# A transformer layer on 8 cores: the weight statistics move into the attention of the first sequence

## The chip, the cores and the metric

The kernel runs on the 8 NeuronCores of one Trainium2 chip. Every core runs the same program on its own 2 of 16 sequences of 2048 tokens (width 1024); the weights are given whole to each core, and the cores never wait for each other. The metric is the device time of the slowest core, in microseconds (us). Each core has TensorE (PE, matmuls), VectorE (DVE), ScalarE (ACT), GpSimd (POOL, here only a queue for DMA writes) and SyncE (SP, here only a queue for DMA loads), which run side by side and meet by semaphores.

## The reference

One pre-norm layer: attention with 16 heads of 64, then a feed-forward part whose two linear maps work on quantized activations and on weights that are quantized to -1, 0 and 1 with one scale for the whole matrix.

```python
x = x + attention(layernorm(x))            # causal, 16 heads
x = x + ffn(layernorm(x))

def weight_quant(w):                       # w1: 4096x1024, w2: 1024x4096, f32
    scale = 1.0 / clip(mean(abs(w)), 1e-05)
    return clip(round(w * scale), -1, 1) / scale
# ffn: h = bit_linear(x, w1); h = silu(conv1d(h, 3 taps)); bit_linear(h, w2)
```

So the scale of a weight needs the mean of |w| over all of its 4 million elements (16 MB) before a single element can be quantized, and the quantized w1 and w2 are needed only in the feed-forward part.

## The kernel before, in words

The program is written out by hand, once for all engines. A recorder (`Rec`) gathers the instructions of each engine, `emit()` plays them into a block, and `barrier()` makes all five engines meet. Within an engine the order in the text is the order of execution. Semaphores count up (`ve` for DVE, `sc` for ACT, `tn` for PE, `dlx`, `dlb` and others for loads), and `wait` names the count that must be reached. All instructions are played by the recorder's one line, L80, so groups of the profile are told apart by the names of tiles.

The stages, each ended by a barrier:

1. Constants; casting the attention weights to bf16 (`p_wst`, `p_wbf`) and writing them to memory.
2. Weight preparation, for w1 and then for w2, in `wprep`. First the statistics: the matrix is loaded in four pieces of 4 MB into one buffer (`wp_st`), ACT takes the absolute value and sums it up (`wp_j`, `wp_as`), and a short chain over DVE, PE and DVE turns it into the mean and its inverse on all partitions (`c_m`, `c_s`). Then the quantization in 8 blocks of 2 MB: load (`wq_st`), scale on ACT (`wq_f`), clip and round on DVE (`wq_b`), 32 transposes on PE (`wq_tp`), copies on DVE (`wq_sp`), and a write by POOL.
3. For each of the two sequences: A, layer norm and the projections Q, K, V (tiles `a_...`). Then B, attention (`b_...`): a bound for the exponentials, then a loop over 4 blocks p of 512 queries and, within it, over 8 head pairs hp. Such a unit of (p, hp) runs over 4(p+1) key blocks kc: PE makes the logits (`b_lp`), ACT the exponential (`b_pt`), on the last four key blocks (the diagonal ones) DVE zeroes a part and multiplies by a triangle (`c_tri`), and PE multiplies by V (`b_av`). At the end of a unit DVE takes a reciprocal (`b_zr`) and makes eight products (`b_at`). After the 8 units of a p come the output projection of its four row tiles v: PE transposes, DVE casts (`b_tt`), PE multiplies, and DVE adds the residual (`b_xr`) into `x2`. Then C, layer norm, activation quantization and the feed-forward part (`c_...`), whose weights are streamed from what stage 2 wrote.

In a unit the order on DVE is: mask of the first diagonal block, then for each further one memset and mask, then reciprocal and products. PE issues the logits of a key block ahead of the value matmuls of the one before. ACT's exponential of a diagonal block past the first waits for the memset. On SP's queue stage B has 16 loads of `b_xr`, of which each past the second waits for the residual sum of two row tiles before.

Of the kernel before, what the change touches and what calls it, by code (L numbers as in the profile page):

```python
# [7 lines left out]
F32 = mybir.dt.float32  # L8
BF16 = mybir.dt.bfloat16
# [5 lines left out]
D = 1024  # L15
NH = 16
DH = 64
HID = 4096
# [73 lines left out]
def build_program(nseq, S):  # L92
# [66 lines left out]
    def barrier():  # L159
        base = bar.v  # L160
        for e in ENGS:
            er = getattr(r, e)
            bar.inc(er.nop() if e in ("sync", "gpsimd") else er.drain())
        for e in ENGS:
            getattr(r, e).wait_ge(bar.sem, base + 5)
# [76 lines left out]
        barrier()  # L242
        r.emit()

    def wprep(t_w, sw_bc, mw_bc, which):
        wn = which
        nel = HID * D
        with nc.sbuf_tensor(f"wp_st{wn}", [128, 8192], F32) as stg, \
             nc.sbuf_tensor(f"wp_j{wn}", [128, 8192], BF16) as junk, \
             nc.sbuf_tensor(f"wp_as{wn}", [128, 4], F32) as asum, \  # L250
             nc.sbuf_tensor(f"wp_s1{wn}", [1, 4], F32) as s1s, \
             nc.psum_tensor(f"wp_ps{wn}", [128, 512], F32) as ups:
            flat = t_w.rearrange("a b -> (a b)").rearrange(
                "(ci p a) -> ci p a", ci=4, p=128)
            for i in range(4):
                b0 = dl.v
                if i > 0:
                    r.wait(r.sync, sc, sc.v)
                dl.inc(r.sync.dma_start(out=stg[:, :], in_=flat[i]), 16)
                r.wait(r.scalar, dl, b0 + 16)  # L260
                sc.inc(r.scalar.activation(junk[:, :], stg[:, :], AF.Abs,
                                           accum_out=asum[:, i:i + 1]))
            r.wait(r.vector, sc)
            ve.inc(r.vector.reduce_sum(asum[:, 0:1], asum[:, 0:4], axis=AX.X))
            r.wait(r.tensor, ve)
            tn.inc(r.tensor.matmul(ups[0:1, 0:1], asum[:, 0:1], onescol[:, :],
                                   start=True, stop=True))
            r.wait(r.vector, tn)
            ve.inc(r.vector.tensor_scalar(s1s[:, 0:1], ups[0:1, 0:1],
                                          1.0 / nel, 1e-5, ALU.mult, ALU.max))  # L270
            ve.inc(r.vector.drain())
            ve.inc(r.vector.reciprocal(s1s[:, 1:2], s1s[:, 0:1]))
            ve.inc(r.vector.drain())
            r.wait(r.tensor, ve)
            tn.inc(r.tensor.matmul(ups[:, 0:1], ones1f[0:1, :], s1s[0:1, 0:1],
                                   start=True, stop=True))
            tn.inc(r.tensor.matmul(ups[:, 1:2], ones1f[0:1, :], s1s[0:1, 1:2],
                                   start=True, stop=True))
            r.wait(r.vector, tn)
            ve.inc(r.vector.tensor_copy(mw_bc[:, :], ups[:, 0:1]))  # L280
            ve.inc(r.vector.tensor_copy(sw_bc[:, :], ups[:, 1:2]))
            r.emit()
            barrier()

        with nc.sbuf_tensor(f"wq_st{wn}", [128, 2 * 4096], F32) as stg2, \
             nc.sbuf_tensor(f"wq_f{wn}", [128, 4096], F32) as qf, \
             nc.sbuf_tensor(f"wq_b{wn}", [128, 4096], BF16) as qb8, \
             nc.sbuf_tensor(f"wq_sp{wn}", [128, 4096], BF16) as strip, \
             nc.psum_tensor(f"wq_tp{wn}", [128, 1024], BF16) as tpp:
            ve_q = 0  # L290
            dw_s = 0
            ve_g = 0
            sc_q = [0, 0]
            for blk in range(8):
                par = blk % 2
# [25 lines left out]
                ve.inc(r.vector.drain())  # L321
                ve_q = ve.inc(r.vector.tensor_scalar(
                    qb8[:, :], qf[:, :], MAGIC, -MAGIC, ALU.add, ALU.add))
                r.wait(r.tensor, ve, ve_q)
                for g in range(4):
                    if not (blk == 0 and g == 0):
                        r.wait(r.tensor, ve, ve_g)
                    for k in range(8):
                        if which == "w1":
                            src_t = qb8[:, (g * 8 + k) * 128:(g * 8 + k + 1) * 128]  # L330
                        else:
                            src_t = qb8[:, k * 512 + g * 128:
                                        k * 512 + (g + 1) * 128]
                        tn.inc(r.tensor.transpose(
                            tpp[:, k * 128:(k + 1) * 128], src_t,
                            ident_bf[:, :]))
                    r.wait(r.vector, tn)
                    ve_g = ve.inc(r.vector.tensor_copy(
                        strip[:, g * 1024:(g + 1) * 1024], tpp[:, :]))
                r.wait(r.gpsimd, ve, ve_g)  # L340
                if which == "w1":
                    dw_s = dw.inc(r.gpsimd.dma_start(
                        out=t_w1t[:, blk].rearrange("hc p h -> p hc h"),
                        in_=strip.rearrange("p (hc h) -> p hc h", hc=32)), 16)
                else:
                    dw_s = dw.inc(r.gpsimd.dma_start(
                        out=t_w2t[blk * 4:(blk + 1) * 4].rearrange(
                            "hl p o -> p hl o"),
                        in_=strip.rearrange("p (hl o) -> p hl o", hl=4)), 16)
            r.wait(r.gpsimd, dw, dw.v)  # L350
            r.emit()
            barrier()

    wprep(t_w1, sw1_bc, mw1_bc, "w1")
    wprep(t_w2, sw2_bc, mw2_bc, "w2")
    r.emit()

    for s in range(nseq):
# [25 lines left out]
        if True:  # L384
# [131 lines left out]
                    f"V{s}": V_sb, f"st24{s}": st24})  # L516
        x2 = es_s.enter_context(
            nc.sbuf_tensor(f"x2_{s}", [128, NT * D], BF16, side="right"))
        es_b = contextlib.ExitStack()
        OWb = es_b.enter_context(nc.sbuf_tensor(f"b_ow{s}", [128, 8192], BF16))  # L520
        Cbias = es_b.enter_context(nc.sbuf_tensor(f"b_cb{s}", [128, 8], F32))
# [7 lines left out]
        if True:  # L529
# [63 lines left out]
            for u in (0, 1):  # L593
                dl_x[u] = dlb[u % 2].inc(r.sync.dma_start(
                    out=xre[:, (u % 2) * D:(u % 2 + 1) * D],
                    in_=t_x[s, u * 128:(u + 1) * 128, :]), 16)
            for p in range(NP):
                kcmax = 4 * (p + 1)
                for hp in range(8):
# [87 lines left out]
                    for hh in range(2):  # L687
                        for qs in range(4):
# [4 lines left out]
                                      ab + hh * 512 + qs * 65 + 64],  # L693
                                zrec[:, hh * 4 + qs:hh * 4 + qs + 1], ALU.mult))
                    ve_pn2[hp % 2] = ve_pn
                for v in range(4):
                    u = 4 * p + v
                    r.wait(r.tensor, ve, ve_pn)
# [32 lines left out]
                    if nu < NT:  # L731
                        r.wait(r.sync, ve, ve_x2)
                        dl_x[nu] = dlb[nu % 2].inc(r.sync.dma_start(
                            out=xre[:, (nu % 2) * D:(nu % 2 + 1) * D],
                            in_=t_x[s, nu * 128:(nu + 1) * 128, :]), 16)
            r.emit()
            barrier()

        es_b.close()
        es_qkv.close()  # L740

        es_c = contextlib.ExitStack()
        xq2 = es_c.enter_context(nc.sbuf_tensor(f"c_xq{s}", [128, 8 * SP2], BF16))
# [539 lines left out]
```

How the kernel before makes its waits and increments, by code:

```python
    def inc(self, h, k=1):  # L30
        h.then_inc(self.sem, k)
        self.v += k
        return self.v
# [6 lines left out]
    def then_inc(self, sem, k):  # L40
        self.entry["incs"].append((sem, k))
        return self
# [27 lines left out]
    def wait(self, engrec, ctr, v=None):  # L70
        if v is None:
            v = ctr.v
        assert v <= ctr.v, "wait on future value -> deadlock"
        if v > 0:
            engrec.wait_ge(ctr.sem, v)
# [2 lines left out]
        def replay(ops, eng):  # L78
            for en in ops:
                h = getattr(eng, en["name"])(*en["args"], **en["kwargs"])
                for sem, k in en["incs"]:
                    h.then_inc(sem, k)
# [76 lines left out]
    def barrier():  # L159
        base = bar.v
        for e in ENGS:
            er = getattr(r, e)
            bar.inc(er.nop() if e in ("sync", "gpsimd") else er.drain())
        for e in ENGS:
            getattr(r, e).wait_ge(bar.sem, base + 5)
```

## Time and profile before

| | us |
|---|---|
| three runs, median (lowest, highest) | 4956.35 (4951.24, 4977.94) |
| the profiled execution | 4969.24 |
| its span, slowest core (core 4) | 4967.7 |
| spans of the eight cores | 4931.2 to 4967.7 |
| stage 1, cast of the attention weights, up to | 176.2 |
| statistics of w1, quantization of w1 | 90.2, 189.5 |
| statistics of w2, quantization of w2 | 83.2, 166.7 |
| sequence 0: A, the bound of B, B, C | 375.2, 99.6, 655.6, 989.5 |

The stages are read from core 4, where the first load of each stage is issued. The span goes from the first to the last instruction of a core; the time of an execution is a little more. Busy time of an engine is time in which it works; DMA-issuing instructions do not count. The granted clock of PE is given as a share of 2.4 GHz, so 0.50 is its lower level of 1.2 GHz. "Idle before" is the time an engine stood ahead of an instruction, with what ended it.

### The profile page before, as it was taken

The page shows a single profiled execution, that of the slowest core. Times are in us where ns is not written, and L with a number is a line of the kernel's source. Part 1 is how long each engine was busy: PE and PEld are TensorE (multiplying, and loading weights), DVE is VectorE, ACT ScalarE, POOL GpSimd, SP SyncE. Part 2 cuts the span into 40 slices and gives each one's busy share as a digit, 9 for nine tenths or more (in the row PEclk, how much of TensorE's full clock was granted, in tenths as well). Part 3 has the DMA queues.
Part 4 walks back from the last instruction along what each step waited for, and adds up shares of the span by engine and source line. Part 5 has one row for each costly group of instructions (what it writes and reads, how often), then busy time and mean ns, then how long its engine had stood idle before and what let it go on. Part 6 is the DMA issues. An engine that isn't in the chain of part 4 may idle for free. (4 is left out here: it accounts for less than half of the span.)

```text
span 4967.7 us, 49356 instructions; the slowest of 8 cores (4931.2 to 4967.7 us)
## 1 busy us (share of the span) xinstructions
PE 2770.6 (56%) x17064; PEld 1414.1 (28%) x17064; DVE 1783.8 (36%) x4539; ACT 1023.7 (21%) x1088; POOL 45.5 (1%) x68
## 2 busy tenths in 40 slices
PE   0011116654667752677766466546677626767765
PEld 0010112211333321444433122113333314444442
DVE  1022232114322136555465221143221365545543
ACT  0122210102344630111100011113446401101010
POOL 0000000000000000000000000000000000000000
PEclk9999998985666565998988889856655659989888
DMA  7563530000000000354544510000000003445444
GB/s 139 180 173 118 195 148 30 17 17 9 18 18 18 1 9 22 70 147 123 147 129 124 190 34 17 17 9 18 18 11 8 9 17 73 136 117 146 119 132 144
DMA packets 468657, 380.91 MB, mean 77 GB/s; under 512 B 340290, under 2 KB 373186, under 8 KB 466372
## 3 DMA queue, kind: packets, MB, share of 16 engines
q1 hardware_dynamic: 457156, 335.81, 23.3%
q0 software_dynamic: 11264, 41.95, 2.6%
q8 instruction: 148, 2.42, 0.2%
q14 instruction: 89, 0.73, 0.1%
HBM read 335.77 MB, written 41.94 MB: 76 GB/s over the span
## 5 line engine op out<-in xcount | busy, mean ns | idle before, releaser
L80 ACT ACTIVATE b_pt<-b_lp,b_cb 128x1024 bf16<-128x1024 f32 (+3 forms) x640 | 622.6, 985 | 611.7 <-PE b_lp L80 393.5
L80 PE MATMUL c_op<-c_w2b,c_hq 128*128 128x512 bf16 x2048 | 526.7, 404 | 273.0 <-DMA c_w2b<-w2t_s 195.3
L80 PE MATMUL c_hp<-c_xq,c_w1b 128*128 128x257 bf16 x4096 | 527.0, 284 | 67.5 <-ACT c_H L80 58.3
L80 PE MATMUL b_av<-V,b_pt 128*128 128x65 bf16 x5120 | 383.7, 241 | 321.9 <-DVE b_pt L80 225.0
L80 PEld LDWEIGHTS b_av<-V,b_pt 128*128 128x128 bf16 x5120 | 296.1, 125 | 618.2 <-issue 618.2
L80 PEld LDWEIGHTS c_hp<-c_xq,c_w1b 128*128 128x128 bf16 x4096 | 412.1, 102 | 209.1 <-issue 108.9
L80 ACT ACTIVATE c_H<-c_hp,c_cb 128x512 bf16<-128x512 f32 x256 | 175.9, 687 | 1275.1 <-DVE c_H L80 734.0
L80 PE MATMUL b_lp<-Q,K 64*128 64x512 bf16 x1280 | 374.6, 602 | 11.0 <-DVE x L80 9.3
L80 PEld LDWEIGHTS c_op<-c_w2b,c_hq 128*128 128x128 bf16 x2048 | 199.0, 101 | 574.7 <-issue 384.6
L80 DVE TENSOR_TENSOR c_H<-c_hp,c_g1b 128x514 bf16<-128x514 f32 x256 | 176.8, 691 | 486.7 <-PE c_hp L80 486.5
L80 DVE TENSOR_TENSOR b_pt<-b_pt,c_tri 128x128 bf16<-128x128 bf16 x512 | 92.5, 222 | 673.0 <-ACT b_pt L80 673.0
L80 PE MATMUL wq_tpw<-c_idb,wq_bw 128*128 128x128 bf16 x512 | 64.7, 306 | 274.6 <-DVE wq_bw L80 228.9
L80 PE MATMUL c_hp<-c_H,c_dg 128*128 128x512 bf16 x768 | 207.5, 379 | 2.0 <-DVE c_H L80 1.0
L80 PE MATMUL wp_psw<-c_oc,wp_asw 128*1 128x1 f32 x4 | 0.4, 163 | 354.2 <-DVE wp_asw L80 354.2
L80 ACT ACT_TABLE_LOAD x14 | 18.0, 1283 | 853.2 <-DMA wp_stw<-w 239.2
L80 PE MATMUL a_vp<-a_vw,a_xh 128*128 128x512 bf16 x512 | 169.3, 490 | 33.2 <-DVE a_xh L80 33.2
L80 DVE TENSOR_SCALAR c_dg<-c_idf,c_cw 128x128 bf16<-128x128 f32 x768 | 171.7, 281 | 21.0 <-PE c_hp L80 10.6
L80 DVE TENSOR_TENSOR c_t<-c_H,c_ss 128x512 f32<-128x512 bf16 x256 | 165.3, 688 | 18.5 <-issue 10.0
L80 PE MATMUL b_lp<-b_ow,b_tt 128*128 128x512 bf16 x512 | 136.3, 414 | 51.7 <-DVE b_tt L80 51.7
L80 PE MATMUL a_qk<-a_xh,a_kw 128*128 128x512 bf16 x512 | 120.8, 378 | 59.4 <-ACT K L80 52.0
L80 PE MATMUL c_tp<-c_idb,c_xm 128*128 128x128 bf16 x256 | 32.4, 307 | 212.3 <-DVEq L80 189.6
L80 PE MATMUL a_qk<-a_xh,a_qw 128*128 128x512 bf16 x512 | 120.6, 379 | 50.4 <-ACT Q L80 50.4
(120 smaller groups left out, 2269.0 us busy)
## 6 DMA issues: line engine op xcount, KB each, us to landing
c_w2b<-w2t_s SPq DMA_DIRECT2D x256, 512.0 KB, 5.4
c_w1b<-w1t_s SPq DMA_DIRECT2D x128, 512.0 KB, 4.4
wp_stw<-w SPq DMA_DIRECT2D x8, 4096.0 KB
wq_stw<-w SPq DMA_DIRECT2D x16, 2048.0 KB, 9.9
a_xt<-x SPq DMA_DIRECT2D x32, 512.0 KB, 3.5
b_xr<-x SPq DMA_DIRECT2D x32, 512.0 KB, 3.5
out<-c_obf POOLq DMA_DIRECT2D x32, 512.0 KB, 3.0
wq_s<-p_wbf POOLq DMA_DIRECT2D x16, 512.0 KB, 7.3
```

Source lines behind the costliest of these rows:

```text
L80: h = getattr(eng, en["name"])(*en["args"], **en["kwargs"])
```

## The change

`wprep` loses its first part and is now `wprep_quant`, with the quantization alone. It is called for both weights behind stage B of sequence 0, ahead of its stage C.

The statistics are taken within stage B of sequence 0. Each weight is read in 16 pieces of 1 MB (128 x 2048 f32), 32 pieces in all, into two buffers (`pw_stg`). Behind the products of each of the 32 units DVE sums |w| of one piece into one column of `pw_as` (`stats_step`) and SP's queue gets the load of the piece after the next (`stats_load`), which waits until its buffer has been summed. The first two loads are issued at the stage's start, behind the two of `b_xr`. Behind stage B's barrier one block makes both means and inverses out of the 32 columns, with more drains than before, and a barrier ends it.

```diff
-    def wprep(t_w, sw_bc, mw_bc, which):
+    def wprep_quant(t_w, sw_bc, mw_bc, which):
-            for i in range(4):
-                b0 = dl.v
-                if i > 0:
-                    r.wait(r.sync, sc, sc.v)
-                dl.inc(r.sync.dma_start(out=stg[:, :], in_=flat[i]), 16)
-                r.wait(r.scalar, dl, b0 + 16)
-                sc.inc(r.scalar.activation(junk[:, :], stg[:, :], AF.Abs,
-                                           accum_out=asum[:, i:i + 1]))
...
-    wprep(t_w1, sw1_bc, mw1_bc, "w1")
-    wprep(t_w2, sw2_bc, mw2_bc, "w2")
...
+            def stats_load(n):
+                if n >= 32:
+                    return
+                par = n % 2
+                if n >= 2:
+                    r.wait(r.sync, ve, pw_abs[n - 2])
+                dlx[2 + par].inc(r.sync.dma_start(
+                    out=pstg[:, par * 2048:(par + 1) * 2048],
+                    in_=pw_flat[n // 16][n % 16]), 16)
+
+            def stats_step(n):
+                par = n % 2
+                r.wait(r.vector, dlx[2 + par])
+                pw_abs[n] = ve.inc(r.vector.reduce_sum(
+                    pasum[:, n:n + 1], pstg[:, par * 2048:(par + 1) * 2048],
+                    axis=AX.X, apply_absolute_value=True))
+                stats_load(n + 2)
...
+            if s == 0:
+                stats_load(0)
+                stats_load(1)
             for p in range(NP):
...
                     ve_pn2[hp % 2] = ve_pn
+                    if s == 0:
+                        stats_step(p * 8 + hp)
                 for v in range(4):
...
         es_b.close()
         es_qkv.close()
+
+        if s == 0:
...
+                for wi, (sw_bc, mw_bc) in enumerate(
+                        ((sw1_bc, mw1_bc), (sw2_bc, mw2_bc))):
+                    nel = HID * D
+                    ve.inc(r.vector.reduce_sum(
+                        pasum[:, 32 + wi:33 + wi],
+                        pasum[:, wi * 16:wi * 16 + 16], axis=AX.X))
...
+                r.emit()
+                barrier()
+            wprep_quant(t_w1, sw1_bc, mw1_bc, "w1")
+            wprep_quant(t_w2, sw2_bc, mw2_bc, "w2")
```

On DVE, at the end of the first unit of p=0 in sequence 0 and the start of the second, the order before is this (`b_zr` and `b_at` end a unit, the rows on `c_tri` are masks):

```order
L80 RECIPROCAL b_zr<-b_av 128x8
L80 TENSOR_SCALAR b_at<-b_av,b_zr 128x64 x8
L80 TENSOR_TENSOR b_pt<-b_pt,c_tri 128x128 x2
L80 MEMSET b_pt 128x2x128
L80 TENSOR_TENSOR b_pt<-b_pt,c_tri 128x128 x2
```

and in the changed kernel this:

```order
L80 RECIPROCAL b_zr<-b_av 128x8
L80 TENSOR_SCALAR b_at<-b_av,b_zr 128x64 x8
L80 TENSOR_REDUCE pw_as<-pw_stg 128x1
L80 TENSOR_TENSOR b_pt<-b_pt,c_tri 128x128 x2
L80 MEMSET b_pt 128x2x128
L80 TENSOR_TENSOR b_pt<-b_pt,c_tri 128x128 x2
```

One reduction stands between a unit's products and the next unit's first mask; the same holds 32 times.

On SP's queue, stage B of sequence 0 holds in the changed kernel:

```order
L80 DMA b_xr<-x 128x1024 x2
L80 DMA pw_stg<-w 128x2048 x10
L80 DMA b_xr<-x 128x1024 x4
L80 DMA pw_stg<-w 128x2048 x8
L80 DMA b_xr<-x 128x1024 x4
L80 DMA pw_stg<-w 128x2048 x8
L80 DMA b_xr<-x 128x1024 x4
L80 DMA pw_stg<-w 128x2048 x6
L80 DMA b_xr<-x 128x1024 x2
```

where the 16 loads of `b_xr` stood alone; the 8 weight loads of a p come ahead of the 4 of its projection.

## Rows read from the trace of the kernel before

**Rows 1.** The profile page: the span.
```profile
span 4967.7 us, 49356 instructions; the slowest of 8 cores (4931.2 to 4967.7 us)
```

**Rows 2.** Timeline of SP's queue (start, us, queue, line, operation, xcount), preparation.
```profile
176.22 66.08 SPq L80 DMA_DIRECT2D wp_stw<-w  x4
266.38 111.49 SPq L80 DMA_DIRECT2D wq_stw<-w  x8
455.92 60.98 SPq L80 DMA_DIRECT2D wp_stw<-w  x4
539.14 99.74 SPq L80 DMA_DIRECT2D wq_stw<-w  x8
705.84 0.35 SPq L80 DMA_DIRECT2D a_qw<-wq_s  x1
```

**Rows 3.** The same timeline on core 5.
```profile
173.39 62.23 SPq L80 DMA_DIRECT2D wp_stw<-w  x4
257.88 111.82 SPq L80 DMA_DIRECT2D wq_stw<-w  x8
447.73 59.90 SPq L80 DMA_DIRECT2D wp_stw<-w  x4
529.63 99.22 SPq L80 DMA_DIRECT2D wq_stw<-w  x8
694.71 0.35 SPq L80 DMA_DIRECT2D a_qw<-wq_s  x1
```

**Rows 4.** Busy time by stage: length, engines (instructions), granted clock, DMA share, GB/s.
```profile
176.22:266.38 90.16, 1.17 (x6) 1.04 (x6) 0.68 (x5) 29.77 (x9) 0.00 (x0) 1.00 0.48 186
266.38:455.92 189.54, 32.36 (x256) 24.74 (x256) 58.84 (x48) 30.95 (x9) 13.53 (x8) 1.00 0.51 133
1180.63:1252.52 71.89, 35.64 (x320) 17.70 (x320) 37.23 (x160) 26.67 (x33) 0.00 (x0) 0.50 0.05 16
1180.63:1836.18 655.55, 452.82 (x3616) 223.32 (x3616) 188.95 (x672) 312.59 (x321) 0.00 (x0) 0.58 0.04 14
```

**Rows 5.** Groups by line: busy us, mean ns, idle before; PE's transposes.
```profile
L80 PE MATMUL wq_tpw<-c_idb,wq_bw 128*128 128x128 bf16 x512 | 64.7, 306 | 274.6 <-DVE wq_bw L80 228.9 <-DVE wq_spw L80 45.6
L80 PE MATMUL c_tp<-c_idb,c_xm 128*128 128x128 bf16 x256 | 32.4, 307 | 212.3 <-DVEq L80 189.6 <-DVE c_xq L80 22.7
```

**Rows 6.** Timeline: reduction chain of w1 on DVE, then ACT's table load.
```profile
263.16 0.16 DVE L80 TENSOR_REDUCE wp_asw<-wp_asw 128x1 f32<-128x4 f32 x1 [92.59 <-ACT wp_jw L80]
265.55 0.15 DVE L80 COPY c_s<-wp_psw 128x1 f32<-128x1 f32 x1
...
547.54 1.28 ACT L80 ACT_TABLE_LOAD   x1 [11.49 <-DMA wq_stw<-w]
```

**Rows 7.** Groups by line: two DVE reductions and a cast.
```profile
L80 DVE TENSOR_REDUCE c_st<-c_xv 128x1 f32<-128x1024 f32 x32 | 36.8, 1211 | 1.1
L80 DVE TENSOR_REDUCE b_sm<-b_ut 8x1 f32<-8x512 f32 x16 | 10.9, 679 | 13.4 <-PE b_ut L80 13.4
L80 DVE CAST p_wbf<-p_wst 128x2048 bf16<-128x2048 f32 x16 | 19.6, 1227 | 124.2 <-DMA wq_s<-p_wbf 115.8 <-DMA p_wst<-qw 8.5
```

**Rows 8.** Timeline of DVE and ACT between the first two units of p=0.
```profile
1190.88 1.63 DVE L80 TENSOR_SCALAR b_at<-b_av,b_zr 128x64 f32<-128x64 f32 x8
1192.42 0.36 DVE L80 TENSOR_TENSOR b_pt<-b_pt,c_tri 128x128 bf16<-128x128 bf16 x2
...
1191.10 1.11 ACT L80 ACTIVATE b_pt<-b_lp,b_cb 128x1024 bf16<-128x1024 f32 x1 [1.88 <-PE b_lp L80]
```

**Rows 9.** Timeline of DVE: ahead of the projection, and in p=1.
```profile
1254.81 1.22 DVE L80 CAST b_tt<-b_av 128x1024 bf16<-128x1024 f32 x1 [2.30 <-PE b_av L80]
...
1305.25 0.36 DVE L80 TENSOR_TENSOR b_pt<-b_pt,c_tri 128x128 bf16<-128x128 bf16 x2 [5.00 <-ACT b_pt L80]
```

**Rows 10.** DMA issues: KB each, median us to landing.
```profile
p_wst<-ow SPq DMA_DIRECT2D x4, 1024.0 KB, 6.4
b_xr<-x SPq DMA_DIRECT2D x32, 512.0 KB, 3.5
```

More of the change, by code:

```diff
@@ L243, in build_program @@
         r.emit()
-    def wprep(t_w, sw_bc, mw_bc, which):
+    def wprep_quant(t_w, sw_bc, mw_bc, which):
         wn = which
[L247 to L254, printed above, removed]
-            for i in range(4):
-                b0 = dl.v
-                if i > 0:
-                    r.wait(r.sync, sc, sc.v)
-                dl.inc(r.sync.dma_start(out=stg[:, :], in_=flat[i]), 16)
-                r.wait(r.scalar, dl, b0 + 16)
-                sc.inc(r.scalar.activation(junk[:, :], stg[:, :], AF.Abs,
-                                           accum_out=asum[:, i:i + 1]))
[L263 to L283, printed above, removed]
         with nc.sbuf_tensor(f"wq_st{wn}", [128, 2 * 4096], F32) as stg2, \
@@ L518, in build_program @@
             nc.sbuf_tensor(f"x2_{s}", [128, NT * D], BF16, side="right"))
+        es_pw = contextlib.ExitStack()
+        if s == 0:
+            pstg = es_pw.enter_context(
+                nc.sbuf_tensor("pw_stg", [128, 2 * 2048], F32, side="right"))
+            pasum = es_pw.enter_context(
+                nc.sbuf_tensor("pw_as", [128, 36], F32, side="right"))
+            pw_flat = [t_w.rearrange("a b -> (a b)").rearrange(
+                "(ci p a) -> ci p a", ci=16, p=128)
+                for t_w in (t_w1, t_w2)]
+            pw_abs = [0] * 32
+            def stats_load(n):
[14 more added lines that the diff above has]
+                stats_load(n + 2)
         es_b = contextlib.ExitStack()
@@ L735, in build_program @@
                             in_=t_x[s, nu * 128:(nu + 1) * 128, :]), 16)
+            if s == 0:
+                for n in range(NP * 8, 32):
+                    stats_step(n)
             r.emit()
@@ L740, in build_program @@
         es_qkv.close()
+        if s == 0:
+            with nc.sbuf_tensor("pw_s1", [1, 8], F32) as s1s, \
+                 nc.psum_tensor("pw_ps", [128, 512], F32) as ups:
+                for wi, (sw_bc, mw_bc) in enumerate(
[4 more added lines that the diff above has]
+                        pasum[:, wi * 16:wi * 16 + 16], axis=AX.X))
+                    ve.inc(r.vector.drain())
+                    r.wait(r.tensor, ve, ve.v)
+                    tn.inc(r.tensor.matmul(
+                        ups[0:1, wi:wi + 1], pasum[:, 32 + wi:33 + wi],
+                        onescol[:, :], start=True, stop=True))
+                    r.wait(r.vector, tn, tn.v)
+                    ve.inc(r.vector.tensor_scalar(
+                        s1s[:, 4 * wi:4 * wi + 1], ups[0:1, wi:wi + 1],
+                        1.0 / nel, 1e-5, ALU.mult, ALU.max))
+                    ve.inc(r.vector.drain())
+                    ve.inc(r.vector.reciprocal(s1s[:, 4 * wi + 1:4 * wi + 2],
+                                               s1s[:, 4 * wi:4 * wi + 1]))
+                    ve.inc(r.vector.drain())
+                    r.wait(r.tensor, ve, ve.v)
+                    tn.inc(r.tensor.matmul(
+                        ups[:, 0:1], ones1f[0:1, :],
+                        s1s[0:1, 4 * wi:4 * wi + 1], start=True, stop=True))
+                    tn.inc(r.tensor.matmul(
+                        ups[:, 1:2], ones1f[0:1, :],
+                        s1s[0:1, 4 * wi + 1:4 * wi + 2],
+                        start=True, stop=True))
+                    r.wait(r.vector, tn, tn.v)
+                    ve.inc(r.vector.tensor_copy(mw_bc[:, :], ups[:, 0:1]))
+                    ve.inc(r.vector.tensor_copy(sw_bc[:, :], ups[:, 1:2]))
+                    ve.inc(r.vector.drain())
+                r.emit()
+                barrier()
+            wprep_quant(t_w1, sw1_bc, mw1_bc, "w1")
+            wprep_quant(t_w2, sw2_bc, mw2_bc, "w2")
+            r.emit()
+        es_pw.close()
         es_c = contextlib.ExitStack()
```

## The prediction

> **What bounds the kernel now.** I read four kinds of view, in this order: the page's head, the issue times on SP's queue (they mark the stages), the busy time of each engine by stage, and the timeline of VectorE (DVE) and ScalarE (ACT) where code is taken out or put in. The span is 4967.7 us on core 4, the slowest [rows 1]. The stages are cut apart by barriers in which all five engines meet, so the kernel is a sum of stages: a stage that shrinks is gained in full, and one that grows is paid in full.
>
> SP's queue shows where the weight preparation lies [rows 2]: statistics of w1 from 176.22 to 266.38 (90.16 us), quantization of w1 to 455.92 (189.54), statistics of w2 to 539.14 (83.22), quantization of w2 to 705.84 (166.70), where the weights of the first projection are loaded. In the statistics ACT works 29.77 us of 90.16, DVE 0.68 and PE 1.17 [rows 4]: four serial loads of 4 MB with one buffer bound them, nothing else. The reader is to see an empty chip here, beside attention of sequence 0 (1180.63 to 1836.18, 655.55 us), in which DVE works 188.95 us and the DMA share is 0.04 [rows 4]. The change lets the second hold the first.
>
> **What is taken out.** Both statistics stages go, with their barriers: 90.16 + 83.22 = 173.4 us on core 4. The same four marks on core 5 are 173.39, 257.88, 447.73 and 529.63 [rows 3], so 84.49 + 81.90 = 166.4 us there. What the slowest core gains lies between; I take 170.
>
> **What moves.** The two quantizations (189.54 and 166.70 us) go behind the attention of sequence 0 and keep code, barriers and order: 0 us. They are a chain of DVE, PE and write latencies between barriers and meet no other work in either place. PE's clock could be the difference: the granted clock reads 1.00 (2.4 GHz) in the first quantization and 0.50 (1.2 GHz) in the first query block of attention [rows 4]. But the transposes tell: `wq_tpw` takes 306 ns in the quantizations, `c_tp`, the same 128x128 bf16 transpose in the stage that follows attention, 307 ns [rows 5]. So PE takes as long for them in either place, and nothing is lost. As a bound: core 5 took 189.85 and 165.08 us for the two [rows 3], core 4 189.54 and 166.70, so they hardly depend on what other cores do at the time; as no trace shows them with cores further apart, I keep 10 us to either side. One instruction goes: the ACT table was swapped for Abs and back, and the second swap back stands at 547.54, 1.28 us, after its data had come [rows 6]. With no Abs between, it goes: -1.3 us. The swap ahead of the first quantization stays. DVE's wait and SP's first load of each stage follow their barrier as before.
>
> **What is added at the end of attention.** The reduction chain (DVE sum, PE over partitions, DVE scale and reciprocal, PE broadcast, two DVE copies) stands from 263.16 to 265.70 for one weight [rows 6], then 0.68 to the next stage's first issue at 266.38. Twice 2.6, a few drains and one barrier: 6.0 us, all on the path, since everybody waits there.
>
> **What is added inside attention.** 32 DVE sums of |w| over 128x2048 f32, one behind the last normalizing product of each of 32 units (4 query blocks p times 8 head pairs hp), with 32 loads of 1 MB.
>
> Price of one: the same operation on 128x1024 f32 takes 1211 ns, on 8x512 679 ns [rows 7]. That is 1.04 ns for each further element, so 1.21 + 1024 x 1.04 = 2.27 us; neighbours overlap by some 0.07, so 2.2 us of the queue. The bound below is the f32 to bf16 cast of the same 2048 elements, 1.227 us [rows 7]; the bound above is twice the 1024 row, 2.42. I take 2.2, because the reduce rows are the same operation. The Trainium skill, "VectorE: DVE Perf Modes", in its table of modes by operation, states that tensor_reduce has only the 1x form; by the trace that holds (1211 ns against 1.227 us for twice the elements in a cast), and by that rule the cast's price, with which the sum would come out 7 us lower (7 x 1.0), can't be had.
>
> Where it is exposed: in p=0 all four key blocks are diagonal, and DVE's triangle mask of the next unit follows the products at once: they start at 1190.88 and last 1.63, ACT's exponential starts at 1191.10 and lasts 1.11, so it ends at 1192.21, and the mask starts at 1192.42 with no idle time noted [rows 8]. A sum put between pushes the mask by its full length; the value matmul waits for the mask, the memset of the next block stands behind it on DVE, and ACT's next exponential waits for that memset. So hp=0 to 6 pay 7 x 2.2 = 15.4 us.
>
> Behind hp=7 of each p comes the output projection. There DVE sat idle 2.30 us waiting for PE's transposes before the cast `b_tt` [rows 9]. PE waits for the products only, which stand ahead of the sum, so 2.2 fits into 2.30: 0 us, with 4 x 0.1 at the edge.
>
> In p=1 to 3 the first 4p key blocks need no mask: DVE is idle 5.00 us before it in p=1 [rows 9], and p=2 and 3 have four and eight more such key blocks ahead of it. 2.2 fits with 2.8 to spare: 24 units less the three hp=7 are 21, 0 us. If that cover weren't there, they would cost 21 x 2.2 = 46 us.
>
> The loads: 1 MB took 6.4 us in the preparation, with writes beside it [rows 10]. A load is issued two units ahead. The shortest unit is that of p=0, (1252.52 - 1180.63) / 8 = 9.0 us [rows 4] (the eighth unit's products end at 1252.52), 11.2 with the sum, so even one load at a time keeps up. The first two are issued behind two loads of 512 KB at the stage's start and the first is wanted 12 us later; I allow 2 us at worst. On SP's queue the loads stand ahead of the residual loads `b_xr` that wait for the projection; each of these is needed two row tiles later and lands in 3.5 us [rows 10], and what is queued ahead has landed by then or has its own slot, so they cost it nothing.
>
> **Sum.** Core 4: -173.4 - 1.3 + 6.0 + 15.4 = -153.3, and 4969.2 (the profiled execution; its span is 4967.7) becomes 4815.9. With 170 taken out: -149.9. The profiled execution is 12.9 us above the median of the three runs, 4956.35, so on the median the forecast is 4956.35 - 149.9 = 4806 us, 3.0% faster.
>
> **Rivals.**
> A. The sums hide in p=0 as well, because something else is late there. For: DVE is busy only 37.23 of 71.89 us in that stretch [rows 4]. Against: the row at 1192.42 has no idle time before it. Time: 4806 - 15 = 4791. Chance 0.04.
> B. The cover in p=1 to 3 fails: a load or a longer sum makes the mask wait. For: ACT, PE and DVE hand work to each other in a tight ring. Against: 5.00 us idle. Time with all 21 exposed: 4806 + 46 = 4852; half of them 4829. Chance 0.08.
> C. The quantizations run slower behind attention (drifted cores, writes against other cores' loads): 10% of 356 us, 36: 4842. Or faster, by the same drift. Against: each is bound by its own chain. Chance 0.06, and the faster side 0.03.
> D. Slower than before: the 32 loads make DVE stand. DVE executes in order, so a load that is late stops masks and with them the attention. For it to eat 150 us, 32 units of a stretch of 655.55 us would have to last (655.55 + 15.4 + 150) / 32 = 25.7 us each on average, so 1 MB would need some 25 us. The row is 6.4. Time past that point, at 30 us a unit: 4806 + 32 x 30 - 671 = 5095. Chance 0.02.
> E. The change doesn't take the time out: the preparation stages shrink but the next barrier waits for something that ran beside them. Nothing did: the window shows 0.68 us of DVE, 1.17 of PE and no POOL in it [rows 4]. Within 0.5% of before: 0.02.
> The forecast itself: 0.75.
>
> **How the numbers follow.** The forecast's own range is 4790 to 4824 (removed 166.4 to 173.4, quantization 10 to either side, p=0 from 8 to 17 us). To hold 8 in 10 I reach into A and half of B: 4786 to 4832. About 0.5% (25 us) is what a measurement tells from no change. Faster by more than that 0.96, within it 0.02, slower 0.02.
>
> **What will show it.** The first load `a_qw` issued near 176 us; 32 `pw_stg` sums of 2.27 us; p=0 of sequence 0 longer by 15 us (71.9 to about 87), p=1 to 3 unchanged; no wait of DVE for `pw_stg`; 6 us from the last residual sum to the first `wq_stw` issue; quantizations of 190 and 165 us. It would be wrong if DVE waited for loads, if the mask in p=1 started late, or if the quantizations changed length.

## The result, and the profile after

The changed kernel takes 4810.93 us, the kernel before 4966.56 (medians of ten runs each). The ratio is 0.9687, with a 95% interval of 0.9667 to 0.9707: between 145 and 165 us faster, 155.6 by the medians. The forecast had -149.9 us and 4806.

The page's head of the kernel after; before, the slowest core had 4967.7 and the fastest 4931.2 [rows 1]:

```profile
span 4798.0 us, 49434 instructions; the slowest of 8 cores (4768.3 to 4798.0 us)
PE 2762.5 (58%) x17064; PEld 1412.6 (29%) x17064; DVE 1853.7 (39%) x4571; ACT 967.2 (20%) x1070; POOL 45.5 (1%) x68
```

SP's queue on core 4 of the kernel after (start, us, queue, line, operation, count) marks its stages, as in [rows 2]:

```profile
180.50 0.35 SPq L80 DMA_DIRECT2D a_qw<-wq_s  x1
...
556.92 0.33 SPq L80 DMA_DIRECT2D b_ow<-wq_s  x1
656.49 0.80 SPq L80 DMA_DIRECT2D b_xr<-x  x2
657.33 88.76 SPq L80 DMA_DIRECT2D pw_stg<-w  x10
755.42 21.42 SPq L80 DMA_DIRECT2D b_xr<-x  x4
794.08 95.54 SPq L80 DMA_DIRECT2D pw_stg<-w  x8
...
1308.01 7.36 SPq L80 DMA_DIRECT2D b_xr<-x  x2
1335.02 296.31 SPq L80 DMA_DIRECT2D wq_stw<-w  x16
```

The first projection's weights are asked for at 180.50 instead of 705.84 [rows 2]: 525 us of preparation stood ahead of it. The quantizations come back at 1335.02. Between the residual loads `b_xr` of two query blocks stand the new `pw_stg` loads, each issued when a sum has freed its half of the buffer.

The stages by engine, core 4 of the kernel after (length; busy us and instructions of PE, weight load, DVE, ACT, POOL; granted clock; DMA share; GB/s): the first query block with its 8 units, the whole attention of sequence 0, and the two quantizations.

```profile
656.49:743.51 87.02, 35.65 (x320) 17.69 (x320) 52.60 (x168) 26.68 (x33) 0.00 (x0) 0.50 0.34 121
656.49:1329.03 672.54, 453.87 (x3616) 223.38 (x3616) 259.15 (x704) 312.39 (x321) 0.00 (x0) 0.58 0.18 63
1335.02:1524.95 189.93, 32.38 (x256) 24.75 (x256) 58.85 (x48) 30.95 (x9) 13.54 (x8) 0.50 0.51 133
1524.95:1698.55 173.60, 32.38 (x256) 24.75 (x256) 58.86 (x50) 30.95 (x9) 6.03 (x8) 0.50 0.43 145
```

Beside [rows 4]: the first block grew from 71.89 to 87.02 (the forecast said about 87), the whole attention from 655.55 to 672.54 us, so +15.1 and +17.0: nearly all that the sums cost, they cost in the first block. DVE's busy time rose by 70.2 us (188.95 to 259.15), of which 53 cost nothing. The quantizations now run at a granted clock of 0.50 (1.2 GHz), where w1's had 1.00 before. On this core w1's needs 189.93 us (189.54 before) and w2's 173.60 (166.70); the 6.9 more of w2's are taken up in the part on the prediction.

The new operation, and PE's transposes of the quantization, in the groups by line (busy us, mean ns, idle before):

```profile
L80 DVE TENSOR_REDUCE pw_as<-pw_stg 128x1 f32<-128x2048 f32 x32 | 72.9, 2277 | 0.0
...
L80 PE MATMUL wq_tpw<-c_idb,wq_bw 128*128 128x128 bf16 x512 | 64.7, 306 | 283.6 <-DVE wq_bw L80 238.3 <-DVE wq_spw L80 45.3
```

The sum lasts 2277 ns, and the 0.0 behind the bar says that DVE never waited for a load. The transposes last 306 ns as before [rows 5], at half the granted clock.

The boundary between two units of the first block, core 4 of the kernel after (start, us, engine, line, operation, idle time before it):

```profile
666.74 1.63 DVE L80 TENSOR_SCALAR b_at<-b_av,b_zr 128x64 f32<-128x64 f32 x8
666.96 1.11 ACT L80 ACTIVATE b_pt<-b_lp,b_cb 128x1024 bf16<-128x1024 f32 x1 [1.88 <-PE b_lp L80]
668.28 2.28 DVE L80 TENSOR_REDUCE pw_as<-pw_stg 128x1 f32<-128x2048 f32 x1
670.48 0.35 DVE L80 TENSOR_TENSOR b_pt<-b_pt,c_tri 128x128 bf16<-128x128 bf16 x2
...
670.97 0.60 PE L80 MATMUL b_av<-V,b_pt 128*128 128x65 bf16 x8 [3.72 <-DVE b_pt L80]
671.20 0.90 ACT L80 ACTIVATE b_pt<-b_lp,b_cb 128x768 bf16<-128x768 f32 x1 [3.13 <-PE b_av L80]
```

The exponential is done at 668.07, but the mask starts at 670.48, because the sum stands before it on DVE. From the products' start the mask is 3.74 us away; before it was 1.54 [rows 8]. The difference is 2.20, the forecast's price, and PE (3.72 us idle, released by DVE's `b_pt`) and ACT (3.13) pay it too. At the same place of the kernel before, core 4, PE had stood idle 1.53 us and ACT 0.94, 2.19 less each:

```profile
1192.93 0.60 PE L80 MATMUL b_av<-V,b_pt 128*128 128x65 bf16 x8 [1.53 <-DVE b_pt L80]
1193.15 0.90 ACT L80 ACTIVATE b_pt<-b_lp,b_cb 128x768 bf16<-128x768 f32 x1 [0.94 <-PE b_av L80]
```

Where the sum was to be hidden, the same core: a unit of p=1, and the cast that opens the projection of p=0.

```profile
745.80 1.22 DVE L80 CAST b_tt<-b_av 128x1024 bf16<-128x1024 f32 x1
...
791.73 2.28 DVE L80 TENSOR_REDUCE pw_as<-pw_stg 128x1 f32<-128x2048 f32 x1
796.82 0.36 DVE L80 TENSOR_TENSOR b_pt<-b_pt,c_tri 128x128 bf16<-128x128 bf16 x2 [2.81 <-ACT b_pt L80]
```

In [rows 9] the mask of p=1 had 5.00 us of idle time ahead of it and the cast 2.30. Of the 5.00 there are 2.81 left and the mask is as early as before; the cast has 0.1 us left (0.21 at the casts of the three later query blocks), so this cover was used up almost to the end.

The loads, 1 MB each, land faster than the 6.4 of [rows 10] (KB each, median us from issue to landing). The residual loads stay at a median of 3.5, which holds for the 16 beside the `pw_stg` loads as well as for the 16 of sequence 1:

```profile
pw_stg<-w SPq DMA_DIRECT2D x32, 1024.0 KB, 4.9
...
b_xr<-x SPq DMA_DIRECT2D x32, 512.0 KB, 3.5
```

The means block, core 7 of the kernel after, DVE; it answers to [rows 6]:

```profile
1334.19 1.22 DVE L80 TENSOR_TENSOR x<-b_xr,b_lp 128x1024 bf16<-128x1024 f32 x1 [4.68 <-PE b_lp L80]
1335.90 0.17 DVE L80 TENSOR_REDUCE pw_as<-pw_as 128x1 f32<-128x16 f32 x1 [0.49 <-PEq L80]
...
1340.68 0.15 DVE L80 COPY c_s<-pw_ps 128x1 f32<-128x1 f32 x1
```

The last residual sum ends at 1335.41, SP issues the first `wq_stw` at 1341.40: 5.99 us for two chains and the barriers ahead of and behind them, forecast 6.0.

From such marks of all eight cores comes the table on which the rest stands: the mean over the cores, in us, of the time to the first `a_qw`; of the middle (from the first residual load of attention of sequence 0 to the first load of feed-forward weights, which holds attention, means and, where they stand there, the quantizations); of the feed-forward stage of sequence 0; and of everything behind the barrier of sequence 1's attention start.

```
kernel             to a_qw   middle   feed-forward 0   sequence 1's rest   span
before              702.7     778.2       867.0             1649.3        4945.8
before, again       705.2     778.4       859.1             1638.5        4926.5
after               181.1    1158.9       860.4             1633.8        4783.8
after, again        179.7    1157.7       857.1             1635.8        4780.2
move_only           348.5    1133.8       865.3             1638.3        4932.8
loads_only          183.7    1143.3       865.7             1637.9        4780.8
sums_late           176.7    1143.2       872.5             1640.2        4780.9
sums_late, again    182.6    1142.9       863.6             1637.3        4774.2
three_p1            175.0    1168.8       848.1             1630.7        4770.6
one_block           177.1    1157.3       853.2             1628.5        4767.4
late_both           181.1    1068.4       859.1             1629.1        4688.3
two_strips          176.5    1038.7       855.6             1638.2        4656.7
all_in              177.1    1037.3       858.4             1631.8        4652.1
```

The projections of q, k, v (372 to 376 us each) and the loads between (99 to 100) are the same in all of them and left out. The column `middle` repeats to about 1 us in two executions of one kernel. The first lies between 175.0 and 183.7 in the ten executions whose kernels start alike. The two feed-forward columns are less steady: two executions of one kernel, before, differ by 19 us in them. So a part of 15 us is read from its own column and not from the total.

### The profile page after: what moved, and what is told of

The parts are those of the page before. It is cut to its first block and busy times, and to the rows that moved or that the text cites. A ratio compares the mean times of both kernels' runs of the same rounds, so it can differ in the third digit from the quotient of the medians.

```text
span 4798.0 us, 49434 instructions; the slowest of 8 cores (4768.3 to 4798.0 us)
## 1 busy us (share of the span) xinstructions
PE 2762.5 (58%) x17064; PEld 1412.6 (29%) x17064; DVE 1853.7 (39%) x4571; ACT 967.2 (20%) x1070; POOL 45.5 (1%) x68
## 5 line engine op out<-in xcount | busy, mean ns | idle before, releaser
L80 PE MATMUL a_tp<-c_idb,a_xm 128*128 128x128 bf16 x256 | 22.3, 238 | 350.0 <-DVE a_xm L80 350.0
L80 ACT ACT_TABLE_LOAD x12 | 15.4, 1283 | 838.8 <-DVE a_st L80 389.0
```

The source lines that it names most:

```text
L80: h = getattr(eng, en["name"])(*en["args"], **en["kwargs"])
```

## Experiments

**before_again: the kernel before once more, unchanged.**

> The kernel before, unchanged: a second profiled execution, to see how far its stages differ from one execution to the next. Theory 1 (the change gains 141 us by its stages and the other 15 to 22 us that the first pair of traces shows in the feed-forward stages are spread between executions): the mean over the cores of the two feed-forward stretches (first w1 load to the next sequence's first load, and attention to the end in sequence 1) moves by 5 to 20 us against the first trace of this kernel (867.0 and 1649.3). Rival theory 2 (the change makes the feed-forward stages faster): they repeat within 3 us, at 867 and 1649, and stay above those of the changed kernel (860.4 and 1633.8).

It took 4947.18 us. The first two columns repeat to 2.5 and 0.2 us, the feed-forward stages of the two sequences do not (867.0 and 859.1, 1649.3 and 1638.5): they moved by 7.9 and 10.8 us with nothing changed, as theory 1 had it. That is the noise in which every later difference has to be seen.

**move_only: the quantizations behind attention, the statistics left at the start.**

```
+    wstats(t_w1, sw1_bc, mw1_bc, "w1")     # the two stages of before, at the start
+    wstats(t_w2, sw2_bc, mw2_bc, "w2")
     ...                                    # no pw_stg, no sums, no means block
```

> Statistics of both weights stay in stages of their own at the start, the two quantizations alone go behind the attention of sequence 0. Theory 1: moving costs and gains nothing, so 0 us against the kernel before (one block boundary more or less, 1 us); quantizations 189 and 166 us in the new place. Rival theory 2: the move itself makes what follows faster, 15 to 20 us below the kernel before. Rival C of the prediction: the quantizations run slower behind attention, up to 36 us above.

Ratio 1.002 (0.9994 to 1.0046), 4970.3 us against 4961.55. SP's queue on core 4 of this kernel shows that the move took place:

```profile
184.95 150.95 SPq L80 DMA_DIRECT2D wp_stw<-w  x8
358.46 0.33 SPq L80 DMA_DIRECT2D a_qw<-wq_s  x1
...
1490.98 292.56 SPq L80 DMA_DIRECT2D wq_stw<-w  x16
```

In the table 355.5 us leave the first column (704.0 to 348.5) and 355.5 come into the second (778.3 to 1133.8). These columns come from one execution and show neither a gain nor a cost. All ten executions together say less plainly that the move is free: the mean span of the eight cores is 4942.2 ± 2.9 us (± is the standard error, here and below), beside 4933.2 ± 1.2 in 13 executions of the kernel before on the same chip. That is 9.0 ± 3.1 more, or 6.5 without the longest of the ten. The profiled execution, with 4932.8, is one of the shortest, so where these us lie isn't shown. The move gives nothing, as forecast, and costs between 0 and some 10 us; the gain is that of the statistics.

**loads_only: all 32 loads, but each sum reads 16 of the 2048 columns (its means are taken over these alone).**

```
-  pasum[:, n:n + 1], pstg[:, par * 2048:(par + 1) * 2048],
+  pasum[:, n:n + 1], pstg[:, par * 2048:par * 2048 + 16],
```

> The changed kernel with all 32 loads of 1 MB, but each sum takes only 16 of the 2048 columns of its piece (the means are therefore taken over fewer elements). Theory 1 (the sums cost, the loads do not): attention of sequence 0 goes back by about 15 us, from 671.9 us to 656 to 658 us (the short sum still costs 0.17 us in each of 7 units), total 15 to 17 us below the changed kernel, near 4795. Rival theory 3 (part of the 17 us is the loads' doing, on the queue or in memory): it goes back by less than 10.

Ratio 0.9671 (0.9618 to 0.9724), 4784.67 us. The sums are down to 158 ns, in the group below; the attention of sequence 0 takes 657.0 us (mean of the cores), against 655.8 before and 671.8 after.

```profile
L80 DVE TENSOR_REDUCE pw_as<-pw_stg 128x1 f32<-128x16 f32 x32 | 5.1, 158 | 0.0
```

So the 32 MB of loads cost about 1 us at most. The seven exposed short sums, 7 x 0.158, explain as much: the first block lasts 72.20 us here and 71.03 in sums_late, which has no sum in it (means of the cores). The 16 us are DVE's time. Rival D, which had the loads at fault, is out.

**sums_late, and again with five rounds: no sum in p=0, one for each unit in p=1, two in p=2 and 3 until all 32 are done.**

```
-  stats_step(p * 8 + hp)
+  for _ in range((0, 1, 2, 2)[p] if hp < 7 else 0):
+      if pw_next < 32:
+          stats_step(pw_next)
+          pw_next += 1
```

> The same 32 sums of full length and loads, but none in the first query block p=0 and none in the last unit of a query block: one per unit in p=1 (7), two per unit in p=2 (14), two per unit in p=3 until all are done (11). Theory 1: where a unit has 5 us idle on DVE ahead of its first mask one sum of 2.2 us is hidden, and where it has 10 and 15 us two are, so all 32 are hidden: attention of sequence 0 at 655 to 657 us and the total 15 to 17 us below the changed kernel, near 4795. Rival: with two in a unit the second waits for its load, or the ring of PE, ACT and DVE is disturbed: gain under 8 us.

> The same kernel as sums_late, now in five rounds on the same chip as the changed kernel: by the attention stage (656.1 against 671.8 us) it should be 16 us, 0.3%, below the changed kernel. Rival: what is won in attention is lost to the spread, and the intervals overlap too far to tell.

The attention of sequence 0 takes 656.1 and 656.5 us, against 671.8 and 671.7 after and 655.8 and 655.9 before: the 16 us are back but for 0.5. DVE on core 4 of this kernel, in p=2:

```profile
951.86 4.47 DVE L80 TENSOR_REDUCE pw_as<-pw_stg 128x1 f32<-128x2048 f32 x2
961.97 0.36 DVE L80 TENSOR_TENSOR b_pt<-b_pt,c_tri 128x128 bf16<-128x128 bf16 x2 [5.63 <-ACT b_pt L80]
```

Two sums, 4.47 us, and 5.63 us of idle time are still left ahead of the mask: the cover in p=2 is 10 us and more. The time of the program, though, is 4796.39 in the one comparison (0.9667, 0.9626 to 0.9709) and 4798.17 in the other (0.969, 0.9659 to 0.972), where the kernel after took 4794.96 on the same chip. By the slowest core the 15 us can't be told, so the rival of the second expectation came out. By the mean span of the cores on that chip (4775.0 ± 4.7, and 4784.5 ± 2.4 after) the gain is 9.5 ± 5.3, which is not clear either. It is the column `middle` (1158.9 and 1157.7 against 1143.2 and 1142.9) that shows it.

**three_p1: three sums instead of one behind each unit of p=1 but the last.**

```
-  stats_step(p * 8 + hp)
+  stats_step(p * 8 + hp, 2 if p == 1 and hp < 7 else 0)   # two extra reductions of the same data
```

> The changed kernel; in the seven units hp=0 to 6 of p=1 of sequence 0 DVE sums each piece three times (the two more sums go to columns that nobody reads). Theory 1 (a sum is free as long as the units' idle time on DVE ahead of the first mask, 5.0 us in p=1, holds it): three sums are 6.6 to 6.7 us, so each of the seven units is longer by 1.6 to 1.8 us and the eight units of p=1 last 11 to 12 us longer than the changed kernel's 113.15, i.e. 124 to 125 us. Rival (the idle time isn't free, the sums are hidden for another reason, or everything past the first sum counts): plus 7 x 4.4 = 31 us. Rival (cover is larger): under 4 us.

This looks for the end of the cover: three sums last 6.66 us, 1.66 more than the 5.00 of [rows 9]. The second block went from 113.15 to 123.87 us, +10.7, that is 1.53 for each of seven units, a little under the 11 to 12 expected (both from the last residual sum of p=0 to the first cast of p=1's projection, mean of the cores). DVE on core 4:

```profile
785.84 6.66 DVE L80 TENSOR_REDUCE pw_as<-pw_stg 128x1 f32<-128x2048 f32 x3
792.41 0.35 DVE L80 TENSOR_TENSOR b_pt<-b_pt,c_tri 128x128 bf16<-128x128 bf16 x2
```

No idle time is noted before the mask any more. So what fitted in free was 6.66 - 1.53 = 5.13 us, the noted idle time of 5.00 to some 0.1 us. The run took 4806.78 us.

**one_block: the two quantizations in one block of the program instead of two.**

```
-            r.emit()
+            if which == "w2":
+                r.emit()
```

> The changed kernel with both quantizations in one block of the program (the barrier between them stays, the block's end between them goes). It asks why ACT's table load ahead of w2's quantization stayed, which the prediction let go. Theory 4 (the load belongs to the first activation of each block of the program, whatever table is in place): 11 table loads in place of 12 and the one near 1535 us is gone, 1.3 us. Theory 5 (it belongs to the change of tables): it is still there. Total within 3 us of the changed kernel either way, which one look can't tell.

The forecast let one table load of ACT go, since Abs was gone. In the kernel after it stands where it stood, core 4, ACT:

```profile
1346.41 1.28 ACT L80 ACT_TABLE_LOAD   x1 [54.07 <-DMA wq_stw<-w]
...
1535.24 1.28 ACT L80 ACT_TABLE_LOAD   x1 [45.53 <-DMA wq_stw<-w]
```

And in this kernel, on its slowest core:

```profile
1351.98 1.28 ACT L80 ACT_TABLE_LOAD   x1 [53.91 <-DMA wq_stw<-w]
...
1542.38 3.71 ACT L80 ACTIVATE wq_fw<-wq_stw,c_s 128x4096 f32<-128x4096 f32 x1 [45.62 <-DMA wq_stw<-w]
```

The first activation of w2 comes without a load, and the page counts 11 loads where the kernel after has 12. The two quantizations use the same activation, so a change of tables can't have asked for the load that stood there. Here it belongs to the first activation of a block of the program, whatever table is in place. 4783.67 us for the run; the gain of 1.3 us is far below what the total can show.

**after_again: the kernel after once more, unchanged, with five rounds.**

> The changed kernel, unchanged, beside the kernel before in five more rounds, and a second profiled execution. Its stages explain 145 us of its gain (statistics gone 170, attention 16 longer, means 6, nothing for the move); 155.6 us were measured. Theory 1 (the rest is spread of the feed-forward stages between executions): the mean span of its cores differs by 5 to 15 us from the first (4783.8), and the gain comes out between 140 and 160 us. Rival theory 2 (the feed-forward stages are faster by the change): again over 155 us.

0.969 (0.9664 to 0.9717), 4794.96 us against 4956.68: -161.7 by these medians. Its stages repeat those of the first run to 1.4 us in the first two columns. Of what theory 1 expected neither figure came: the mean span of the profiled execution moved by 3.6 us (4783.8 to 4780.2) instead of 5 to 15, and 161.7 lies above 160, on the side of the rival that has the feed-forward stages faster by the change. The mean span of the cores over these executions (11 before, 6 after) decides: it fell by 148.5 ± 3.3 us, where the stages explain 145 and the rival needs 15 to 20 more. A gain of a few us in feed-forward is not excluded.

**late_both: as sums_late, and DVE's wait for the write of the strip later, where the strip is first written.**

```
-                if blk > 0:
-                    r.wait(r.vector, dw, dw_s)      # ahead of the clip
...
+                    if blk > 0 and g == 0:
+                        r.wait(r.vector, dw, dw_s)  # ahead of the first strip copy
```

> The 32 sums placed as in sums_late, and in the quantizations the wait of DVE for the write of the block before is moved from ahead of clip and round, which do not touch the strip that is being written, to ahead of the first copy into the strip. Theory: the wait (8.8 us in w1, 5.4 to 6.8 in w2) stood in a row with clip, round and the first transposes (6.0 us together) and now stands beside them: a block of w1 takes 15.4 in place of 21.7 us and one of w2 13.5 in place of 19.3, so 7 x 6.3 + 7 x 5.8 = 85 us less, near 4796 - 85 = 4711. Rival: the loads of 2 MB in pieces of 512 bytes beside the writes become the bound and half of it is lost, 4750.

Ratio 0.9507 (0.9443 to 0.9571), 4706.99 us, forecast 4711. The quantizations were never the change's subject, but they are the longest idle stretch left: the clip of the next block waited for the previous block's write though it touches other data. In the kernel after, core 4:

```profile
1372.93 2.29 DVE L80 TENSOR_SCALAR wq_fw<-wq_fw 128x4096 f32<-128x4096 f32 x1 [8.86 <-DMA w1t_s<-wq_spw]
```

With the wait moved, core 4 of this kernel:

```profile
1375.21 2.29 DVE L80 TENSOR_SCALAR wq_fw<-wq_fw 128x4096 f32<-128x4096 f32 x1
1375.86 2.95 POOL L80 DMA_DIRECT2D w1t_s<-wq_spw  x1 [14.69 <-DVE wq_spw L80]
1377.64 3.26 DVE L80 TENSOR_SCALAR wq_bw<-wq_fw 128x4096 bf16<-128x4096 f32 x1
...
1385.38 0.69 DVE L80 COPY wq_spw<-wq_tpw 128x1024 bf16<-128x1024 bf16 x1 [4.48 <-DMA w1t_s<-wq_spw]
```

The wait is now 4.48 us and stands behind the clip, the rounding and the first transposes. The middle is 74.6 us shorter than with sums_late alone, where 85 were expected. In w1 the clips of two blocks stand 16.5 to 17.6 us apart on core 4 past the first pair, instead of the 15.4 expected; 1.0 us of each is a rounding that got longer (3.26 us in place of 2.29 in the rows above), which the last section takes up. In w2 they stand 13.1 to 14.3 apart past the first pair, with 13.5 expected.

**two_strips: as late_both, with two strip buffers in turn, each with its own counter.**

```
+             nc.sbuf_tensor(f"wq_sp{wn}", [128, 2 * 4096], BF16) as strip2, \
...
+                    if blk > 1 and g == 0:
+                        r.wait(r.vector, dwq[par], dw_s2[par])
```

> As late_both, and with two strips, so that a block's copies wait only for the write of the block before the last. Theory: no wait for writes is left and DVE and PE are the bound with 4.8 (clip, round) + 1.2 (first transposes) + 6.6 (copies) = 12.7 us a block: against late_both another 7 x 2.7 + 7 x 0.8 = 25 us, near 4686. Rival: the DMA engines are the bound (share 0.51 of a 21.7 us block is 11.1 us of work for w1) and w1 stays at 14 us or more.

Ratio 0.945 (0.9375 to 0.9525), 4677.11 us, forecast 4686. The middle goes down by another 29.7 us, to 1038.7, where 25 were expected. The strip copies in the groups by line (behind the bar the idle time before them, with the releasers) show where it came from; first late_both:

```profile
L80 DVE COPY wq_spw<-wq_tpw 128x1024 bf16<-128x1024 bf16 x64 | 44.3, 692 | 114.8 <-PE wq_tpw L80 63.2 <-DMA w1t_s<-wq_spw 32.2 <-DMA w2t_s<-wq_spw 19.4
```

and two_strips:

```profile
L80 DVE COPY wq_spw<-wq_tpw 128x1024 bf16<-128x1024 bf16 x64 | 44.3, 692 | 83.7 <-PE wq_tpw L80 83.7
```

No copy waits for a write any more, and the idle time is 31.1 us less on these cores, about the gain of the middle.

**all_in: two_strips and one_block together.**

> two_strips with both quantizations in one block of the program, as in one_block: one table load (1.3 us) and one block's end less. Expected 1 to 3 us below two_strips, 4675, which is 5.7 to 5.8% below the kernel before; the version that should beat both kernels.

Ratio 0.9416 (0.9393 to 0.9438), 4668.46 us (five rounds): 288 us less than the kernel before on the same chip (4956.68), and the fastest kernel of the case. In its profiled execution the spans of the cores lie between 4644.0 and 4658.8. The middle is 1037.3, 1.4 less than with two_strips, about the length of one table load (1.28).

## Why the prediction was right

**Statistics out, -170.** The time to `a_qw` went from 704.0 (mean of both executions of before) to 179.1 (mean of the ten runs whose kernel starts like the one after), -524.9; without the 355.5 of the quantizations, which move_only shows to be the whole of what moved, this is -169.4. The step holds, the middle value between cores 4 and 5 was the right choice, and rival E (the time does not come out) is out.

**The move, 0.** It holds to within some 10 us, the margin it was given. The ratio of move_only is 1.002 (0.9994 to 1.0046), and the transposes last 306 ns at a granted clock of 0.50 as at 1.00. But the mean span of move_only's cores is 9.0 ± 3.1 us longer, and in the kernel after the two quantizations took 359.1 and 358.1 us in its two executions (mean of the cores), against 355.5 and 354.8 before: some 3 us more, which is rival C on a small scale. The difference lies in w2's. On core 4 it took 173.60 us and on core 7 166.5, with the same busy time of DVE. The waits of its seven clips for the write of the block before are (us in total, times, longest), core 4 and then core 7:

```profile
DVE wq_fw L80 <- DMA w2t_s<-wq_spw: 50.0, 7, 8.3
...
DVE wq_fw L80 <- DMA w2t_s<-wq_spw: 43.7, 7, 6.7
```

These are 6.3 of the 7.1 us between the two cores. Why the writes of core 4 land later stays open.

**The table load, -1.3.** This step failed. I had read the second load as a switch back from Abs; it is placed at the first activation of a block of the program, and stayed (one_block: 12 loads with two blocks, 11 with one). The Trainium skill, "ScalarE: Activation LUTs", section "What ACT_TABLE_LOAD costs", measures the load at about 1283 ns and, with a drain, gives about 2.66 us "for every switch to a different set". The 1283 ns agree with each load in these traces. That without a switch there is no load, which is how I had taken it, does not hold.

**The means, +6.0.** The stretch from the last residual sum to the first `wq_stw` is 5.99 us, as forecast. But it holds the barrier behind attention, which the kernel before has too: in move_only, without the means, the same stretch is 0.45 us (mean of the cores). So 5.5 were added.

**The sums in p=0, +15.4.** 89.32 against 74.19 us (mean of the cores, from the first residual load to the projection's first cast) is +15.1, from a sum of 2277 ns where 2.27 us was worked out from two shorter reductions. A unit of p=0 lasts 8.45 us before and 10.64 after, 2.19 more; two or three units of each kernel are 0.3 longer than that, in different places, and this wasn't looked into. The whole attention is +16.1 (655.76 to 671.84) and +15.8 in the second executions; the last 1.0 lies in p=1 to 3 and their projections, in which no single part moved by more than 0.6. Rival A asked for a mask that can start later for free; the row at 670.48 shows that it can't. The rule taken from "VectorE: DVE Perf Modes" of the Trainium skill, that tensor_reduce has only the 1x form, held: 1.04 ns for each further element up to 2048.

**The cover in p=1 to 3, 0.** A row and two runs speak for it: 2.81 us left of 5.00, 656 us of attention with all sums in p=1 to 3, and +10.7 us as soon as the sums were made longer than the cover. Rival B is out, with a reserve that is now known: 2.8 us for a unit in p=1, and 7.8 in p=2 (5.63 and one sum).

**The sum, and the slowest core.** The two columns give -524.9 + 380.0 (middle, 778.3 to 1158.3) = -144.9 us. The measured figures are those of the slowest core, and spread more. Over all executions on record that list the span of each core, from several chips, the mean span of the eight cores was 4930.6 ± 1.8 us before (32 executions) and 4789.2 ± 1.5 after (17), a difference of 141.4 ± 2.3. On the one chip of after_again it was 148.5 ± 3.3. So the columns account for the mean of the cores to some 4 us.

The slowest core gained more: 155.6 by the first medians, 155.3 by the means of after_again's executions (147.9 with all chips thrown together, 4956.8 and 4808.9). The time of an execution stood 26.2 ± 1.9 us above the mean of its cores before and 19.7 ± 1.8 after, which is the rest; whether the change narrows the spread of the cores was not tested.

The forecast's gain of 149.9 is 5.0 larger than that of the columns. With both executions of each kernel, its steps were too good by 1.3 (table load), 3.1 (quantizations), 0.5 (whole attention) and 0.6 (statistics) and too bad by 0.5 (means), together 5.0. That it still comes out 5.7 below the measured 155.6 is luck in part: the slowest core's extra gain, which it did not consider, outweighs what its steps had missed. Its own range of 4790 to 4824 is not quite the sum of its terms, which give 4786 to 4822; nothing hangs on that.

What was not foreseen is where more was to be had. The forecast called the quantizations a chain between barriers and left them alone; nearly a third of that chain was one wait, placed ahead of the clip though only the strip copies need it. In the kernel after it comes to 106.5 of 359 us on core 7 (62.8 in w1, 43.7 in w2). Moving it and giving it a second buffer brought 104 us, two thirds of what the change itself brought.

## What to carry to other kernels

The idle time that the timeline notes ahead of the next instruction on an engine was here the room for work put there, to little more than a tenth of a microsecond: 2.2 us were free ahead of an idle 5.00, 6.66 cost 1.5, and where no idle time stood the whole 2.2 was paid by three engines. Put filler work first where that room is widest (here the later query blocks), not where the loop happens to start. And when a stage is a chain, look at what each wait guards before moving the stage: a wait belongs ahead of the first instruction that touches the buffer.

## What the runs showed of the hardware

DVE and POOL slowed each other where a DVE pass over f32 in SBUF and POOL's DMA issue coincided. Core 0 of all_in (start, us, engine, operation):

```profile
1369.64 2.28 DVE L80 TENSOR_SCALAR wq_fw<-wq_fw 128x4096 f32<-128x4096 f32 x1
1370.27 2.96 POOL L80 DMA_DIRECT2D w1t_s<-wq_spw  x1 [10.64 <-DVE wq_spw L80]
1372.06 3.26 DVE L80 TENSOR_SCALAR wq_bw<-wq_fw 128x4096 bf16<-128x4096 f32 x1
```

The groups by line of the kernel after, where the two never meet, have 2294 ns for the rounding `wq_bw` and 1692 for the issue:

```profile
L80 DVE TENSOR_SCALAR wq_bw<-wq_fw 128x4096 bf16<-128x4096 f32 x16 | 36.7, 2294 | 2.2
...
L80 POOL DMA_DIRECT2D w1t_s<-wq_spw x8 | 13.5, 1692 | 1329.7 <-DVE wq_spw L80 1329.7
```

Side by side the issue begins under the clip and ends 1.31 us after it (1371.92 to 1373.23), and the rounding, begun before the issue's end, ends 2.09 us after it, 0.97 later than it would alone. The Trainium skill, "SBUF — State Buffer", section "Who interferes with whom", says that a DVE operation in a two-port mode and GpSimd hold one shared pair of ports in turn, each for its whole instruction, while the other is fully blocked. The order of ends agrees with taking turns; a part of the blocked instruction seems to run all the same, since 1.31 and 2.09 us are less than the 1.69 and 2.29 that each needs alone.

The price is an estimate of 7 x 0.97, some 7 us, over w1's seven overlapping blocks. In w2 the issue is shorter (0.75 us alone); it took 1.96 beside the clip, and the rounding kept its 2.29. The clips of two_strips, core 4, bear it out: past the first pair they stand 13.5 to 14.0 us apart in w1 and 12.6 to 12.8 in w2. That is far less than the wait it came with.

The granted clock of 0.50 against 1.00 changed nothing for transposes of 128x128 that are eight in a row between DVE copies (306 ns in both), so for these transposes the low clock was no loss to look for.
